# Layer 0's attention: scores one head at a time, and each product with v cut into two pieces that lie in two steps

## The chip, the cores and the metric

The kernel runs on one core of one Trainium2 chip. The metric is the device time in microseconds of one execution, and the median of three executions is quoted.

## What is computed

Two transformer layers on a (2, 1024, 128) input; attention and a feed-forward part are added in parallel in each. The change touches the attention of layer 0 alone:

```python
x = L0_attn_x
xn = _layernorm(x, axis=-1)
x = x + _L0_attn_ref(xn, ...) + _L0_ffn_ref(xn, ...)
xn = _layernorm(x, axis=-1)
x = x + _L1_attn_ref(xn, ...) + _L1_ffn_ref(xn, ...)

# _L0_attn_ref: B, T, C = 2, 1024, 128; H = 16 heads of D = 8
qkv = x @ W_attn + b_attn
att = jnp.einsum('bhtd,bhsd->bhts', q, k) / jnp.sqrt(D)
att = att + _alibi_causal_mask(T, H, x.dtype)[None]
att = jax.nn.softmax(att, axis=-1)
y = jnp.einsum('bhts,bhsd->bhtd', att, v)
return y.reshape(B, T, C) @ W_proj + b_proj
```

## The kernel before

Layer 0's attention is done in 8 groups (2 batches, 4 heads each at a time). A group has 10 units, UNITS, and each unit is one step of a loop of 80 steps; the text calls a group's steps u0 to u9. u0 to u2 make the first 512 queries, u3 to u9 the last 512. A unit holds up to 512 columns of queries against one block of 128 keys: u0 and u3 to u7 have one segment of 512, u1 and u8 have two (384 and 128), u2 and u9 one of 256.

In a step TensorE computes the scores of the group's 4 heads (`scores`, line 651, bf16; q and k carry the ALiBi terms and the row maximum as extra rows, 55 in all). Heads 0 and 2 lie in rows 0 to 63 of the array, heads 1 and 3 in rows 64 to 127, so that two neighbours can run side by side. The scores go to three PSUM banks in turn: score k of the whole run uses bank k % 3 and waits until exponential k - 3 has been read. ScalarE takes the exponential of each score (line 1402) into `prob`, which has 3 slots, GpSimd sets what lies above the diagonal to zero (line 1533), and `pv` multiplies the result with v (line 669, float32, 16 output rows for each head, the four heads in four column strips of the array), always into bank 7. After u2 and after u9 `acc` has ScalarE copy bank 7 to `yacc` (line 1391). The next product, that of u3 or u0, overwrites bank 7 and waits for that copy (`s_acc`).

Beside this each step has items from a list (ITEMS, in general two for a step, one for each half of the step) that work one group ahead. A max item is a round of score products for the row maximum (line 583, and line 587 in the two of nine rounds that hold the diagonal) into two of four further banks, which VectorE reduces (line 1088). Item k waits for the reduction of item k - 2. A group has 18 max items. A turn item transposes the finished maxima (line 635), ScalarE copies them to `mrow` (line 1356), and the sync engine writes them with four DMAs into q_op (line 471, `load_m`). Turn (n, 0) lies in u5, turn (n - 1, 1) in u1. Behind the four DMAs of turn (n, 0) the same queue issues the four loads of q_op and k_op for the group after it (line 463, `load_ops`), and for these the first max item of that group waits, which lies in u9. In the last group there are no max items; the tail's items (transposes, projection) lie beside its steps.

The engines' instructions stand in program order, written out by hand in one function for each engine; only semaphores order them against one another. SyncE's queue carries all DMAs.

Of the kernel before, what the change touches and what calls it, by code (L numbers as in the profile page):

```python
# [22 lines left out]
P = 128  # L23
# [9 lines left out]
GH = 4  # L33
# [74 lines left out]
P_SLOTS = 3  # L108
# [70 lines left out]
def build(nc, x, w, wright, consts, alibi_q, alibi_k, masks, chosen, out):  # L179
    alibi_q, alibi_k, masks, chosen = (v.bitcast(BF16) for v in (alibi_q, alibi_k, masks, chosen))  # L180
    with ExitStack() as ctx:
# [340 lines left out]
        def _(pe):  # L522
# [33 lines left out]
            def item(k):  # L556
# [14 lines left out]
                elif kind == "max":  # L571
# [8 lines left out]
                    for t, (i, j, nb, at) in enumerate(ROUNDS[r]):  # L580
                        for odd in range(2):
                            rows = rows_of(odd, MAX_K)
                            last = mm(PS[:, ring + odd, P * at:P * (at + nb)], q_op[rows, slot, pair, P * i:P * i + P],  # L583
                                      k_op[rows, slot, pair, P * j:P * (j + nb)], start=(t == 0), stop=(r not in DIAGONALS),
                                      skip_group_check=True)
# [71 lines left out]
            def pv(s):  # L657
                n, u = divmod(s, NU)
                b, g = GROUPS[n]
                half, segs = UNITS[u]  # L660
                pe.wait_ge(s_exp, GH * (s + 1))
                pe.wait_ge(s_tri, TRI[s])
                if u in (0, 3):
                    pe.wait_ge(s_acc, 1 + 2 * n + (u == 3))
                at = 0
                for j, i0, nn in segs:
                    c0 = P * i0 - SPAN * half
                    for h in range(GH):
                        last = mm(PS[STRIP * h:STRIP * h + VW, 7, c0:c0 + nn], vaug[:, TPB * b + j, g * GH + h, :],  # L669
                                  prob[:, s % P_SLOTS, h, at:at + nn], start=(j == 0),  # L670
                                  stop=(u in (2, 9)), skip_group_check=True)
                    at += nn
                last.then_inc(s_pv, 1)
# [47 lines left out]
            for s in range(NSTEP + 1):  # L721
                beside = items_of_step(s) if s < NSTEP else ()
                for half in range(2):
                    if s < NSTEP:
                        scores(s, range(GH // 2 * half, GH // 2 * (half + 1)))
                    for k in (beside[:len(beside) // 2], beside[len(beside) // 2:])[half]:
                        item(k)
                if s:
                    pv(s - 1)
# [580 lines left out]
        def _(a):  # L1310
# [82 lines left out]
            for s in range(NSTEP + 1):  # L1393
# [4 lines left out]
                for half in range(2):  # L1398
                    for h in range(GH // 2 * half, GH // 2 * (half + 1)) if s < NSTEP else ():
# [3 lines left out]
                                       ACT.Exp).then_inc(s_exp, 1)  # L1403
                    for k in (beside[:len(beside) // 2], beside[len(beside) // 2:])[half]:
                        item(k)
                if s:
                    acc(s - 1)
# [272 lines left out]
```

## Time and profile before

| what | value |
|---|---|
| median of 3 runs | 536.89 us (532.29 to 537.02) |
| profiled execution: time, span | 539.22 us, 537.5 us |
| TensorE busy (x4188) | 424.8 us, 79% |
| VectorE busy (x584) | 351.0 us, 65% |
| ScalarE busy (x471) | 241.2 us, 45% |
| GpSimd busy (x309) | 195.6 us, 36% |
| mean granted clock of TensorE | 0.939 |
| line 1402, exponentials, x320 | 159.9 us busy, 73.5 us idle before them |
| line 1088, reductions of maxima, x144 | 171.9 us busy, 49.8 us idle before them |
| line 669, products with v, x768 | 83.7 us busy |
| line 651, scores, x384 | 61.7 us busy, 43.8 us idle before them |

The attention of layer 0 lies between about 43 and 304 us of the span, 80 steps. Busy times are unions for each engine and a mean over stages; matmuls are pipelined, and each float32 matmul stands as two records.

### The profile page before, as it was taken

To read this page: it belongs to the slowest core of one execution; us is meant where nothing else is said; L and a number is where in the kernel's file an instruction comes from. 1 tells how busy PE (TensorE), PEld (TensorE's weight loads), DVE (VectorE), ACT (ScalarE), POOL (GpSimd) and SP (SyncE) were. 2 spreads that over 40 slices of the span, in tenths; PEclk is the share of its full clock that TensorE was granted. 3 is DMA by queue.
4 is the path that set the end of the run, shared out by engine and by line. 5 is a ranking of instruction groups with operands and counts; after the bars stand their busy time and mean duration, and the time that the engine had idled before them with its cause. 6 is when DMAs were issued, how large, how long until landed. Compare 5 with 4: busy or idle time off the path is not lost.

```text
span 537.5 us, 10677 instructions
## 1 busy us (share of the span) xinstructions
PE 424.8 (79%) x4188; PEld 197.1 (37%) x4188; DVE 351.0 (65%) x584; ACT 241.2 (45%) x471; POOL 195.6 (36%) x309
## 2 busy tenths in 40 slices
PE   6797788878788787788686896596888798869766
PEld 3253213232222222221242552344544463446544
DVE  5878768778788878786255285876368627862640
ACT  1575476877776777767566210431111111121220
POOL 3022515252322222130210146638338716780530
PEclk9997789999999999998799597888999998999989
DMA  7632240414202020200000032221022102300000
GB/s 225 225 77 68 78 159 16 169 30 164 64 3 66 2 68 2 67 2 2 2 1 1 1 117 79 79 80 41 1 79 99 40 2 79 119 21 1 22 3 20
DMA packets 19094, 31.92 MB, mean 59 GB/s; under 512 B 2544, under 2 KB 7120, under 8 KB 18724
## 3 DMA queue, kind: packets, MB, share of 16 engines
q1 hardware_dynamic: 19044, 31.23, 18.1%
q8 instruction: 34, 0.56, 0.4%
q14 instruction: 16, 0.13, 0.1%
HBM read 13.20 MB, written 8.06 MB: 40 GB/s over the span
## 4 chain that ended last, share of the span: by engine, by line
PE 35%; issue 18%; POOL 18%; ACT 10%; DVE 8%; DMA 6%; SPq 5%; POOLq 0%; ACTq 0%; DVEq 0%
PE PS L669 9%; ACT prob L1402 7%; PE PS L651 6%; POOL vdec L1562 6%; POOL qr L1554 5%; POOL xn L1571 5%; DVE pmax L1088 4%; DMA k_op<-k_scr 4%; SPq L471 3%; PE PS L583 3%; PE PS L587 2%; PE PS L784 2%; POOL kr L1554 1%; PE PS L540 1%; PE PS L880 1%
## 5 line engine op out<-in xcount | busy, mean ns | idle before, releaser
L1088 DVE TENSOR_REDUCE pmax<-PS 128x8 f32<-128x1024 f32 x144 | 171.9, 1222 | 49.8 <-PE PS L583 33.4
L1402 ACT ACTIVATE prob<-PS 128x512 f32<-128x512 f32 (+1 forms) x320 | 159.9, 552 | 73.5 <-PE PS L651 70.5
L1533 POOL TENSOR_SCALAR_AFFINE_SELECT prob<-prob 128x512 f32<-128x512 f32 x64 | 39.9, 635 | 179.7 <-ACT prob L1402 179.7
L651 PE MATMUL PS<-q_op,k_op 55*128 55x512 bf16 (+3 forms) x384 | 61.7, 342 | 43.8 <-ACT prob L1402 41.1
L669 PE MATMUL PS<-prob,vaug 128*16 128x512 f32 (+3 forms) x768 | 83.7, 526 | 0.0
L583 PE MATMUL PS<-k_op,q_op 52*128 52x128 bf16 (+3 forms) x576 | 58.5, 279 | 9.1 <-DVE pmax L1088 4.6
L651 PEld LDWEIGHTS PS<-q_op,k_op 55*128 55x128 bf16 x384 | 18.4, 94 | 125.4 <-ACT prob L1402 108.7
L1571 POOL TENSOR_TENSOR xn<-state,c_sb 128x512 f32<-128x512 f32 x28 | 29.3, 1046 | 81.5 <-DVE state L1271 56.4
L1426 ACT COPY vk<-PS 128x512 f32<-128x512 f32 x16 | 9.4, 585 | 86.5 <-PE PS L795 86.5
L784 PE MATMUL PS<-xnT,w_sb 128*128 128x512 f32 x80 | 44.0, 650 | 0.6 <-DVE by_sin L1238 0.6
L1554 POOL TENSOR_TENSOR qr<-qr,turned 128x512 f32<-128x512 f32 x32 | 40.0, 1269 | 4.9 <-DMA turned<-by_sin 4.8
L1271 DVE TENSOR_TENSOR state<-PS,xn 128x512 f32<-128x512 f32 x28 | 19.3, 688 | 30.4 <-PE PS L864 21.5
L1562 POOL TENSOR_TENSOR vdec<-vk,c_sb 128x256 f32<-128x256 f32 x64 | 37.2, 613 | 1.4 <-ACT vk L1426 1.4
L1457 ACT COPY oT<-PS 128x512 f32<-128x512 f32 x32 | 17.2, 589 | 39.0 <-PE PS L853 39.0
L583 PEld LDWEIGHTS PS<-k_op,q_op 52*128 52x128 bf16 x576 | 24.8, 96 | 22.8 <-DVE pmax L1088 9.4
L1234 DVE TENSOR_TENSOR qr<-PS,c_sb 128x512 f32<-128x512 f32 x32 | 21.9, 683 | 13.0 <-PE PS L784 12.9
L1245 DVE TENSOR_TENSOR sm<-PS,c_sb 128x512 f32<-128x512 f32 x32 | 20.6, 685 | 13.8 <-PE PS L812 13.1
L812 PE MATMUL PS<-qr,kr 64*64 64x256 f32 x256 | 19.2, 414 | 12.4 <-DVE state L1271 6.3
L880 PE MATMUL PS<-oT,w_sb 128*128 128x256 f32 x128 | 28.7, 382 | 0.0
L836 PE MATMUL PS<-sm,vk 64*64 64x256 f32 x256 | 19.7, 426 | 11.0 <-DVE sm L1245 11.0
L669 PEld LDWEIGHTS PS<-prob,vaug 128*16 128x16 f32 x768 | 15.2, 97 | 34.5 <-ACT prob L1402 21.7
L1238 DVE TENSOR_TENSOR by_sin<-PS,c_sb 128x512 f32<-128x512 f32 x40 | 27.1, 678 | 0.0
(181 smaller groups left out, 527.2 us busy)
## 6 DMA issues: line engine op xcount, KB each, us to landing
turned<-by_sin SPq DMA_DIRECT2D x80, 128.0 KB, 2.0
k_op<-k_scr SPq DMA_DIRECT2D x14, 220.0 KB
q_op<-q_scr SPq DMA_DIRECT2D x14, 208.0 KB
c_sb<-const_dram SPq DMA_DIRECT2D x1, 2060.0 KB, 7.2
w_sb<-w_dram SPq DMA_DIRECT2D x1, 1876.5 KB, 7.6
q_scr<-part_a SPq DMA_DIRECT2D x6, 256.0 KB, 3.5
k_scr<-part_a SPq DMA_DIRECT2D x6, 256.0 KB, 3.8
q_scr<-part_b SPq DMA_DIRECT2D x6, 256.0 KB, 3.4
```

Source lines behind the costliest of these rows:

```text
L583: last = mm(PS[:, ring + odd, P * at:P * (at + nb)], q_op[rows, slot, pair, P * i:P * i + P], k_op[rows, slot, pair, P * j:P * (j + nb)], ...
L651: last = mm(PS[:, (GH * s + h) % ST_BANKS, at:at + nn], k_op[rows, slot, h // 2, P * j:P * j + P], q_op[rows, slot, h // 2, P * i0:P * i0 ...
L669: last = mm(PS[STRIP * h:STRIP * h + VW, 7, c0:c0 + nn], vaug[:, TPB * b + j, g * GH + h, :], prob[:, s % P_SLOTS, h, at:at + nn], start=( ...
L784: mm(bank01(("p", i, m)), w, xnT[:, SPAN * i:SPAN * i + SPAN], start=True, stop=True).then_inc(s_pj, 1)
L880: last = mm(by_half(ps)[:, :, s, :], wo[:, C * kt:C * kt + C], by_half(oT[:, i % 2, kt, :])[:, :, s, :], start=False, stop=(s == 1 and kt ...
L1088: vec.tensor_reduce(pmax[:, of_pair, at:at + step * (TPS - 1) + 1:step], both.rearrange("p a (b c) -> p a b c", c=P), AX.X, ALU.max).then_ ...
L1238: vec.tensor_tensor(by_sin[:, n % SIN_SLOTS, :], PS[:, k % 2, :], K["sin"][:, t], ALU.mult).then_inc(s_pj_free, 1)
L1402: sca.activation(prob[:, s % P_SLOTS, h, 0:UNIT_W[u]], PS[:, k % ST_BANKS, 0:UNIT_W[u]], ACT.Exp).then_inc(s_exp, 1)
L1533: po.affine_select(out=blk, in_=blk, compare_op=ALU.is_ge, fill=0.0, base=0, pattern=[[0, GH], [1, P]], channel_multiplier=-1).then_inc(s_ ...
L1554: po.tensor_tensor(dst, dst, turned[:, n % TURN_SLOTS, :], ALU.add).then_inc(done, 1)
L1562: po.tensor_tensor(vdec[:, c % 2, g, :, :], vk[:, c % 2, D1 * g:D1 * g + D1].rearrange("p (o e) -> p o e", o=1).broadcast_to([P, HPG, D1]) ...
L1571: po.tensor_tensor(faded, state[:, u % STATES, :, :], fade, ALU.mult).then_inc(s_faded, 1)
```

## The change

TensorE's step is written in another order. Before: scores of heads 0 and 1, the first item, scores of heads 2 and 3, the second item, the whole product with v of the step before. Now: score 0, first item, score 1, the second piece of the product of two steps ago, score 2, second item, score 3, the first piece of the product of the step before. A product of two segments is cut between them, one of a single segment in the middle of its columns (256 and 256, or 128 and 128). The products of a max item take the odd head first: ahead of the item stands an even head's score, behind it an odd head's. ScalarE's copy of bank 7 for step s - 2 stands behind the exponential of head 2 of step s; before, the copy for step s - 1 stood at the end of step s. The loops run one step longer.

```diff
@@ item(), TensorE
-                        for odd in range(2):
+                        for odd in (1, 0):
...
@@ pv(), TensorE
-            def pv(s):
+            def pv(s, piece):
...
-                pe.wait_ge(s_exp, GH * (s + 1))
-                pe.wait_ge(s_tri, TRI[s])
-                if u in (0, 3):
-                    pe.wait_ge(s_acc, 1 + 2 * n + (u == 3))
-                at = 0
-                for j, i0, nn in segs:
+                if piece == 0:
+                    pe.wait_ge(s_exp, GH * (s + 1))
+                    pe.wait_ge(s_tri, TRI[s])
+                    if u in (0, 3):
+                        pe.wait_ge(s_acc, 1 + 2 * n + (u == 3))
+                j, i0, nn = segs[0]
+                pieces = segs if len(segs) == 2 else [(j, i0, nn // 2), (j, i0 + nn // 2 // P, nn // 2)]
+                at = pieces[0][2] if piece else 0
+                for j, i0, nn in pieces[piece:piece + 1]:
...
-                last.then_inc(s_pv, 1)
+                if piece:
+                    last.then_inc(s_pv, 1)
@@ the loop over steps, TensorE
-            for s in range(NSTEP + 1):
+            for s in range(NSTEP + 2):
...
-                        scores(s, range(GH // 2 * half, GH // 2 * (half + 1)))
+                        scores(s, [GH // 2 * half])
                     for k in (beside[:len(beside) // 2], beside[len(beside) // 2:])[half]:
                         item(k)
-                if s:
-                    pv(s - 1)
+                    if s < NSTEP:
+                        scores(s, [GH // 2 * half + 1])
+                    at, piece = ((s - 2, 1), (s - 1, 0))[half]
+                    if 0 <= at < NSTEP:
+                        pv(at, piece)
@@ the loop over steps, ScalarE
+                        if h == 2 and s >= 2:
+                            acc(s - 2)
...
-                if s:
-                    acc(s - 1)
+                if s >= NSTEP:
+                    acc(s - 2)
```

TensorE before, u6 and the start of u7 of a group: two scores (L651), a max item on the diagonal (L583, L587), two scores, a max item, the product with v (L669).

```order
L651 MATMUL PS<-q_op,k_op 128x512 [waits s_exp]
L651 MATMUL PS<-q_op,k_op 128x512
L583 MATMUL PS<-k_op,q_op 128x128 [waits s_used0]
L583 MATMUL PS<-k_op,q_op 128x128 x7
L587 MATMUL PS<-masks_sb 128x512 x2
L651 MATMUL PS<-q_op,k_op 128x512 [waits s_exp]
L651 MATMUL PS<-q_op,k_op 128x512
L583 MATMUL PS<-k_op,q_op 128x512 [waits s_used1]
L583 MATMUL PS<-k_op,q_op 128x512
L669 MATMUL PS<-prob,vaug 16x512 [waits s_tri,s_exp]
L669 MATMUL PS<-prob,vaug 16x512 x3
L651 MATMUL PS<-q_op,k_op 128x512 [waits s_exp]
```

TensorE now, at the same place (the product with v is L673):

```order
L651 MATMUL PS<-q_op,k_op 128x512 [waits s_exp]
L583 MATMUL PS<-k_op,q_op 128x128 [waits s_used0]
L583 MATMUL PS<-k_op,q_op 128x128 x7
L587 MATMUL PS<-masks_sb 128x512 x2
L651 MATMUL PS<-q_op,k_op 128x512 [waits s_exp]
L673 MATMUL PS<-prob,vaug 16x256 x4
L651 MATMUL PS<-q_op,k_op 128x512 [waits s_exp]
L583 MATMUL PS<-k_op,q_op 128x512 [waits s_used1]
L583 MATMUL PS<-k_op,q_op 128x512
L651 MATMUL PS<-q_op,k_op 128x512 [waits s_exp]
L673 MATMUL PS<-prob,vaug 16x256 [waits s_tri,s_exp]
L673 MATMUL PS<-prob,vaug 16x256 x3
```

Each score stands alone now, and a piece of 256 columns stands behind the second and the fourth.

TensorE before, in u1: the turn item (L635), two scores in two segments, a max item, the product of u0 with its wait for the copy of bank 7 (`s_acc`), the next step's first score.

```order
L635 MATMUL PS<-masks_sb,mpart 12x128 [waits s_mpart,s_used1]
L635 MATMUL PS<-masks_sb,mpart 12x128 x3
L651 MATMUL PS<-q_op,k_op 128x384 [waits s_exp]
L651 MATMUL PS<-q_op,k_op 128x384
L651 MATMUL PS<-q_op,k_op 128x128 x2
L583 MATMUL PS<-k_op,q_op 128x128 [waits s_used0]
L583 MATMUL PS<-k_op,q_op 128x128
L583 MATMUL PS<-k_op,q_op 128x384 x2
L669 MATMUL PS<-prob,vaug 16x512 [waits s_acc,s_tri,s_exp]
L669 MATMUL PS<-prob,vaug 16x512 x3
L651 MATMUL PS<-q_op,k_op 128x256 [waits s_exp]
```

TensorE now, from the piece of u9 that follows the second score of u1 to the first score of u2:

```order
L673 MATMUL PS<-prob,vaug 16x128 x4
L651 MATMUL PS<-q_op,k_op 128x384 [waits s_exp]
L651 MATMUL PS<-q_op,k_op 128x128
L583 MATMUL PS<-k_op,q_op 128x128 [waits s_used0]
L583 MATMUL PS<-k_op,q_op 128x128
L583 MATMUL PS<-k_op,q_op 128x384 x2
L651 MATMUL PS<-q_op,k_op 128x384 [waits s_exp]
L651 MATMUL PS<-q_op,k_op 128x128
L673 MATMUL PS<-prob,vaug 16x256 [waits s_acc,s_tri,s_exp]
L673 MATMUL PS<-prob,vaug 16x256 x3
L651 MATMUL PS<-q_op,k_op 128x256 [waits s_exp]
```

The wait for `s_acc` stands at the same place of u1 as before, at its end, but the product that the copy reads ends in the middle of u1 now, where it ended with u0 before.

ScalarE before, u0, u1 (`prob` are the exponentials, `mrow` the turned maxima, `yacc` the copy of bank 7):

```order
L1402 ACTIVATE prob<-PS 128x512 [waits s_st,s_pv]
L1402 ACTIVATE prob<-PS 128x512 [waits s_st] x3
L1391 COPY yacc<-PS 128x512 [waits s_pv]
L1402 ACTIVATE prob<-PS 128x512 [waits s_st,s_pv]
L1402 ACTIVATE prob<-PS 128x512 [waits s_st]
L1356 COPY mrow<-PS 12x512 [waits s_item]
L1402 ACTIVATE prob<-PS 128x512 [waits s_st] x2
```

ScalarE now, the same two steps:

```order
L1409 ACTIVATE prob<-PS 128x512 [waits s_st,s_pv]
L1409 ACTIVATE prob<-PS 128x512 [waits s_st] x3
L1409 ACTIVATE prob<-PS 128x512 [waits s_st,s_pv]
L1409 ACTIVATE prob<-PS 128x512 [waits s_st]
L1363 COPY mrow<-PS 12x512 [waits s_item]
L1409 ACTIVATE prob<-PS 128x512 [waits s_st]
L1398 COPY yacc<-PS 128x512 [waits s_pv]
L1409 ACTIVATE prob<-PS 128x512 [waits s_st]
```

The copy of bank 7 has moved from ahead of u1's first exponential to behind its third, and behind the copy of the maxima.

## Rows read from the trace of the kernel before

**Rows 1.** Waits, 40 to 305 us: engine, line <- releaser: total us, times, longest

```profile
ACT prob L1402 <- PE PS L651: 70.5, 86, 4.1
PE PS L651 <- ACT prob L1402: 41.1, 62, 3.4
...
PE PS L583 <- DMA k_op<-k_scr: 2.8, 4, 1.0
```

**Rows 2.** Timeline of TensorE in u6: start us, us, what, [idle before <- releaser]

```profile
190.04 0.39 PE L583 MATMUL PS<-k_op,q_op 52*128 52x128 bf16 x8
...
191.04 0.39 PE L651 MATMUL PS<-q_op,k_op 55*128 55x512 bf16 x2
191.25 0.40 PE L583 MATMUL PS<-k_op,q_op 52*128 52x512 bf16 x2
191.58 1.05 PE L669 MATMUL PS<-prob,vaug 128*16 128x512 f32 x8
192.56 0.39 PE L651 MATMUL PS<-q_op,k_op 55*128 55x512 bf16 x2
```

**Rows 3.** Timeline of ScalarE, u0 to u5 of the sixth group

```profile
201.86 2.24 ACT L1402 ACTIVATE prob<-PS 128x512 f32<-128x512 f32 x4 [0.93 <-PE PS L651]
204.38 0.58 ACT L1391 COPY yacc<-PS 128x512 f32<-128x512 f32 x1 [0.28 <-PE PS L669]
204.87 1.09 ACT L1402 ACTIVATE prob<-PS 128x512 f32<-128x512 f32 x2
205.83 0.56 ACT L1356 COPY mrow<-PS 12x512 bf16<-12x512 bf16 x1
...
207.52 0.66 ACT L1402 ACTIVATE prob<-PS 128x256 f32<-128x256 f32 x2 [0.17 <-PE PS L651]
...
213.34 2.27 ACT L1402 ACTIVATE prob<-PS 128x512 f32<-128x512 f32 x4
216.12 1.08 ACT L1402 ACTIVATE prob<-PS 128x512 f32<-128x512 f32 x2 [0.51 <-PE PS L651]
217.09 0.56 ACT L1356 COPY mrow<-PS 12x512 bf16<-12x512 bf16 x1
```

**Rows 4.** Timeline of VectorE, from u9 of the fifth group on

```profile
200.13 3.49 DVE L1088 TENSOR_REDUCE pmax<-PS 128x8 f32<-128x1024 f32 x3 [1.40 <-PE PS L587]
```

**Rows 5.** Chain of waits, u6 to u9 of the fifth group

```profile
193.16 5.79 DMA k_op<-k_scr
...
199.09 0.40 PE PS L583 x8
```

**Rows 6.** Timeline of TensorE: the DMA's wait in u9 of the sixth group

```profile
227.90 0.40 PE L583 MATMUL PS<-k_op,q_op 52*128 52x128 bf16 x8 [0.98 <-DMA k_op<-k_scr]
```

**Rows 7.** Timeline of TensorE in the last group: a product of 256 columns, the next scores

```profile
276.35 0.63 PE L669 MATMUL PS<-prob,vaug 128*16 128x256 f32 x8
...
276.91 0.39 PE L651 MATMUL PS<-q_op,k_op 55*128 55x512 bf16 x2
```

**Rows 8.** Timeline of ScalarE in the last group, u3 and u4

```profile
274.26 2.24 ACT L1402 ACTIVATE prob<-PS 128x512 f32<-128x512 f32 x4 [1.76 <-PE PS L651]
...
277.52 2.24 ACT L1402 ACTIVATE prob<-PS 128x512 f32<-128x512 f32 x4
```

**Rows 9.** Stretches: length, busy us (x) of PE, PEld, DVE, ACT, POOL; PEclk, DMA

```profile
225.00:230.00 5.00, 3.91 (x48) 1.43 (x48) 3.33 (x4) 2.86 (x7) 2.57 (x8) 1.00 0.25 57
...
242.90:246.30 3.40, 3.38 (x15) 0.44 (x16) 1.66 (x2) 1.45 (x3) 0.00 (x0) 0.50 0.00 0
...
260.00:265.00 5.00, 4.16 (x29) 2.18 (x27) 0.00 (x0) 2.68 (x5) 0.19 (x1) 0.50 0.01 2
```

**Rows 10.** Timeline of TensorE, just ahead of the last stretch of rows 9

```profile
259.81 0.37 PE L635 MATMUL PS<-masks_sb,mpart 128*12 128x128 bf16 x3 [1.67 <-POOL mpart L1510]
```

**Rows 11.** Timeline of ScalarE, u4 and u5 of the seventh group

```profile
242.15 1.12 ACT L1402 ACTIVATE prob<-PS 128x512 f32<-128x512 f32 x2
...
246.43 1.08 ACT L1402 ACTIVATE prob<-PS 128x512 f32<-128x512 f32 x2 [1.80 <-PE PS L651]
```

More of the change, by code:

```diff
@@ L669, in pv @@
                         last = mm(PS[STRIP * h:STRIP * h + VW, 7, c0:c0 + nn], vaug[:, TPB * b + j, g * GH + h, :],
-                                  prob[:, s % P_SLOTS, h, at:at + nn], start=(j == 0),
+                                  prob[:, s % P_SLOTS, h, at:at + nn], start=(j == 0 and piece == 0),
                                   stop=(u in (2, 9)), skip_group_check=True)
-                    at += nn
-                last.then_inc(s_pv, 1)
+                if piece:
+                    last.then_inc(s_pv, 1)
             def unit_b(k, part):
@@ L1391, in acc @@
                     sca.copy(yacc[:, n, SPAN * half:SPAN * half + SPAN], PS[:, 7, :]).then_inc(s_acc, 1)
-            for s in range(NSTEP + 1):
+            for s in range(NSTEP + 2):
                 u = s % NU
```

## The prediction

> **What bounds the kernel now.** First I read the page, then the waits, then one step on TensorE, then the engines that hand work to one another, last the chain of waits at the seams between groups. In the attention no engine is full. ScalarE waits 70.5 us for scores and TensorE 41.1 us for exponentials [rows 1]: each waits for the other in turn. The reader is to see the loop in one step [rows 2]. Scores of heads 2 and 3 start at 191.04, the second item 0.21 us later, the product with v at 191.58, and it holds TensorE until the next step's scores at 192.56, 0.98 us. ScalarE needs 2.24 us for four exponentials; in a plain step 0.51 us of idle stand in front of its first exponential [rows 3], so it takes 2.75 us, and this idle is what the block costs. That is what the change can win: with the block halved and scores spread evenly, three banks are enough for ScalarE, and the next limit is VectorE with two reductions a step, 3.49 us for three or 1.16 us each [rows 4], so 2.33 us.
>
> The reader is to see a second loop as well, at the seam between groups. In u5 ScalarE copies the turned maxima, and only then does the queue issue four DMAs and four loads; the last load takes 5.79 us, and the first max item of the group after, in u9, starts at 199.09 [rows 5]. From the copy at 217.09 [rows 3] to the same item at 227.90 [rows 6] it is 10.8 us. TensorE stood still for this DMA in four groups, up to 1.0 us each [rows 1]. So in those groups the steps u5 to u9 are already as long as the DMA chain allows, and faster steps there only make that wait longer. What counts for them is the other part of the round: from the item in u9 (199.09) to the copy in u5 (217.09), 18.0 us.
>
> **The price of cutting a product.** A product of 256 columns takes 0.56 us up to the next scores, one of 512 takes 0.98 [rows 2, 7]. So two halves cost 1.12, 0.14 more. A piece that follows an item starts 0.33 us behind the item's start, scores that precede an item only 0.21 [rows 2]: going over from scores to the product costs 0.12, and there is one more such passage. Together TensorE gets 0.26 us more for each step. A plain step is then 0.21 + 0.33 + 0.56, twice, or 2.2 us, and is hidden by VectorE's 2.33; a step with an item on the diagonal has 0.45 more (scores follow such an item at most 1.0 us behind its start, 190.04 to 191.04 [rows 2], with a wait in it; I take 0.87, less the overlap of a score) and is bound by TensorE at 2.65.
>
> The Trainium skill says in TensorEngine Tiling, Key Properties, that a change of the tiling mode drains the engine. Scores use the array in two row halves, the products in four column strips, so the change doubles these drains; the 0.12 and 0.14 above agree with such a drain and give it a size. Without it, with 0.26 less in each of u9, u0 and u2 of seven groups, the forecast would be some 4 us lower.
>
> The swapped order of the odd and the even head costs nothing in itself: the score ahead runs beside the item's first product, the score behind beside its last. If a bank isn't free, the item's last product runs alone, 0.21 us, which lies in a wait anyway.
>
> **The copy of bank 7.** The product of u0 (and of u3) must wait for the copy of bank 7. Before, that copy was made at the end of u0, a whole step ahead of the product at the end of u1. Now it stands behind the third exponential of u1, and the product still stands at the end of u1. From u1's first exponential, the copy of the maxima starts at 0.96 and takes 0.56, the third exponential starts some 1.42 behind the first and takes 0.55, the copy itself 0.58 [rows 3]: its end is at 2.55 us; with 0.12 to pass it on, the piece starts at 2.7. TensorE is there about 0.9 us after that first exponential, since score 3 only needs the first one to be read. It stands still for almost 2 us, with the piece (0.56), the next step's first score and its max item queued behind the wait; ScalarE runs dry meanwhile (0.5 us), and VectorE too. In u4 there is no copy of maxima, the wait is some 1.4 us, and the step is 2.25 + 0.12 + 0.56 + 0.49 (scores to first exponential) = 3.4 us against 2.78 before (213.34 to 216.12).
>
> **The seam, walked through.** From the item in u9 as zero, with these prices, the first exponential of u0 comes at 3.4 (before 2.77), of u1 at 5.9 (5.78: the copy is no longer ahead of it), of u2 at 9.5 (8.43), of u3 at 12.6, of u4 at 14.8 (14.25), of u5 at 18.2 (17.03) [all "before" from rows 3, less 199.09]. The copy of the maxima comes at 19.2 against 18.0: **+1.2 us** a group, at the one stretch that the DMA chain doesn't cover.
>
> **The sum.**
> - Stretch u9 to u5: five rounds of the DMA loop x 1.2 = +6.0, and the groups outside it (first, seventh) about +1.1 each: +8.2.
> - u5 to u9 where no load is waited for (first and seventh group): 2.7 + 2.65 + 2.33 + 2.33 + 2.6 = 12.65 us against four plain steps of 2.75 and a shorter u9, about 13.4: -0.75 x 2 = -1.5. In the fourth group VectorE has the feed-forward's scales beside its reductions: nothing.
> - Last group: no reductions, steps near 3.26 (274.26 to 277.52 [rows 8]). TensorE waits for a bank in them and could fill that with a piece, some 0.4 in five of the steps, but pays 0.26 and the wait for the copy twice: -1.
> - TensorE's clock. In u9 TensorE would wait for the loads some 2.2 us in place of 1.0, in u1 almost 2 us for the copy. The trace has a wait of 1.67 us [rows 10], and the granted clock stands at 0.5 (1.2 GHz) right behind it [rows 9]; behind the 1.0 us of the DMA wait at 227.90 it stayed at 2.4 GHz [rows 6, 9]. With the lower level from 242.9 to 246.3 [rows 9] u4 of the seventh group took 4.3 us, 242.15 to 246.43 [rows 11], against 2.78, so one fall costs about 1.5. There are eleven places (four DMA waits, seven u1); I count four falls and take off the one that stands in the trace now: +4.5. Bounds: -1.5 (none) to +15 (all).
>
> Total +10.2. The profiled execution took 539.2 us, 2.3 above the median; set on the median 536.9 this gives **547 us**.
>
> **Rivals.**
> - *The same waits, but the clock holds.* +5.7, 542.6 us (539 to 545). For it: the waits of up to 1.0 us in the steps now leave the clock at 2.4 GHz, 225 to 230 among them [rows 9]. Against: the wait of 1.67 us and what came behind it [rows 9, 10].
> - *Faster: the wait for the copy is hidden.* If ScalarE is far enough ahead when TensorE comes to the piece (because TensorE itself is late, with drains dearer than 0.12, or the items held up by VectorE), u1 and u4 lose nothing, and the stretch u9 to u5 goes down toward VectorE's work: 11 reductions x 1.16 + 2.5 for the start and the turn items = 15.3 in place of 18.0. A third to all of these 2.7 us seven times, with -1.5 and -1: 515 to 528 us, say 524. It decides where TensorE reaches the piece less than 0.5 us ahead of the copy's end. Against: score 3 waits only for exponential 0 of its step, and behind it nothing stands before the piece.
> - *Nothing that counts moves.* The DMA loop holds the round, the wait for the copy costs what the spread scores win in u0 to u4: +0 there, -1.5 and -1: 534 us.
> - *Half clock that stays.* If TensorE's work in u9 to u2 at the lower level takes the whole time, one fall brings the next: over 553 us.
>
> **Chances.** Forecast 0.45 (541 to 553), clock holds 0.22, hidden wait 0.17, nothing moves 0.12, half clock that stays 0.04. A measurement tells 1% (5.4 us, 531.5 to 542.3) from no change. The clock case lies across the upper bound, half on each side; that makes slower 0.58, same 0.26, faster 0.16. The range leaves out the hidden wait and the lasting half clock: 532 to 554.
>
> **What would show it.** Behind the copy of bank 7 in u1 and u4 a product with v waits for ScalarE's line of that copy, about 1.9 and 1.4 us (none of that before): right. Steps u6 to u8 near 2.3 to 2.65 us, against 2.75: the mechanism of the spread scores. The wait of TensorE for the loads in u9 up from 1.0 to some 2.2 us, and 30 us from such an item to the next (28.8 before, 199.09 to 227.90): the DMA loop. A mean granted clock below 0.939. I am wrong if the round between two such items falls below 28.5 us, if the product isn't seen waiting for the copy, or if steps stay at 2.75.

## The result, and the profile after

The changed kernel is **slower: 549.98 us** against 536.95 us of the kernel before on the same chip, ratio 1.027 (95% interval 1.021 to 1.033). A second measurement on another chip gave 1.025 (1.016 to 1.034). Its profiled execution took 553.81 us with a span of 552.1 us, 14.6 us above the profiled span before. Ratios here leave out executions more than 1.5% above the fastest of their kernel, so they differ by up to a per cent or so from the quotient of two medians.

The page of the changed kernel, busy times, the granted clock in 40 slices of the span, and the groups of the exponentials (L1409), of the product with v (L673) and of the scores (L651):

```profile
PE 460.7 (83%) x4700; PEld 216.6 (39%) x4700; DVE 349.9 (63%) x584; ACT 243.8 (44%) x471; POOL 195.9 (35%) x309
...
PEclk9997589989999998989789897898999999989958
...
L1409 ACT ACTIVATE prob<-PS 128x512 f32<-128x512 f32 (+1 forms) x320 | 164.0, 558 | 86.8 <-PE PS L651 84.6
L673 PE MATMUL PS<-prob,vaug 128*16 128x256 f32 (+2 forms) x1280 | 99.8, 386 | 15.2 <-ACT yacc L1398 14.9
L651 PE MATMUL PS<-q_op,k_op 55*128 55x512 bf16 (+3 forms) x384 | 106.6, 345 | 3.5 <-ACT prob L1409 2.8
```

VectorE and ScalarE do the same work as before; TensorE is busy 36 us longer, and ScalarE still waits for scores, longer than before. The scores' own busy time, 61.7 us before, is 106.6 us now: scores that had run side by side, two at a time, now come one at a time. The waits view of the changed kernel, 40 to 320 us (engine, line <- releaser: total, times, longest), answers to [rows 1]:

```profile
ACT prob L1409 <- PE PS L651: 84.6, 107, 3.2
...
PE PS L673 <- ACT yacc L1398: 14.9, 14, 1.3
```

TensorE's wait for exponentials, 41.1 us in [rows 1], is all but gone. In its place stands a wait that did not exist: the product with v waits for the copy of bank 7, 14 times. TensorE's timeline of the changed kernel, from u9 of the fifth group to u9 of the sixth (start, us, what, idle before and its releaser):

```profile
206.65 0.40 PE L583 MATMUL PS<-k_op,q_op 52*128 52x128 bf16 x8 [1.39 <-DMA k_op<-k_scr]
...
207.72 1.02 PE L673 MATMUL PS<-prob,vaug 128*16 128x256 f32 x8
...
216.85 0.62 PE L673 MATMUL PS<-prob,vaug 128*16 128x256 f32 x8 [1.30 <-ACT yacc L1398]
...
225.00 0.62 PE L673 MATMUL PS<-prob,vaug 128*16 128x256 f32 x8 [0.98 <-ACT yacc L1398]
...
228.17 0.39 PE L651 MATMUL PS<-q_op,k_op 55*128 55x512 bf16 x1
...
230.12 0.39 PE L651 MATMUL PS<-q_op,k_op 55*128 55x512 bf16 x1
...
231.22 0.39 PE L651 MATMUL PS<-q_op,k_op 55*128 55x512 bf16 x1
...
232.32 0.39 PE L651 MATMUL PS<-q_op,k_op 55*128 55x512 bf16 x1
...
237.33 0.40 PE L583 MATMUL PS<-k_op,q_op 52*128 52x128 bf16 x8 [1.43 <-DMA k_op<-k_scr]
```

A plain step takes 2.20 us (230.12 to 232.32, from the third score of u6 to that of u7), and u6 as a whole, with its item on the diagonal, 3.05 us (228.17 to 231.22). But u1 and u4 stand still behind the copy, and both items in u9 wait longer for the loads than in [rows 6]. The piece at 207.72 takes 1.02 us where its like takes 0.62: the clock had fallen (a granted clock of 0.52 from 207.7 to 211). ScalarE's timeline, u1 and u5 of the same group:

```profile
215.20 0.56 ACT L1363 COPY mrow<-PS 12x512 bf16<-12x512 bf16 x1
215.66 0.58 ACT L1409 ACTIVATE prob<-PS 128x512 f32<-128x512 f32 x1
216.15 0.56 ACT L1398 COPY yacc<-PS 128x512 f32<-128x512 f32 x1
...
227.11 0.56 ACT L1363 COPY mrow<-PS 12x512 bf16<-12x512 bf16 x1
```

The copy of bank 7 ends at 216.71 and the piece starts 0.14 us behind it. In the rest of the text a **round** is the time from one copy of bank 7 after u9 to the next; the second round begins with the first such copy, at 87.51 before and 93.18 now, and the stretch ahead of it is called the first. The stretches view (length, busy us of PE, PEld, DVE, ACT, POOL, then granted clock, DMA share, GB/s) of the kernel before: the third, the sixth and the seventh round, and the part behind the attention, which the change doesn't touch:

```profile
115.92:145.08 29.16, 23.76 (x242) 7.82 (x240) 24.19 (x23) 21.50 (x44) 10.63 (x25) 1.00 0.33 106
204.38:233.19 28.81, 22.67 (x234) 6.99 (x232) 22.07 (x21) 21.50 (x44) 7.30 (x19) 1.00 0.12 32
233.19:266.93 33.74, 26.08 (x218) 8.40 (x216) 18.89 (x21) 22.08 (x46) 7.62 (x19) 0.85 0.01 2
...
303.48:537.50 234.02, 184.06 (x2128) 112.48 (x2128) 134.78 (x284) 42.12 (x78) 114.89 (x133) 0.94 0.14 51
```

The same of the changed kernel:

```profile
123.90:154.06 30.16, 26.64 (x304) 9.77 (x304) 24.10 (x23) 21.69 (x45) 10.17 (x23) 1.00 0.31 103
...
216.15:246.83 30.68, 26.97 (x296) 9.20 (x296) 21.92 (x21) 21.81 (x45) 7.31 (x18) 0.94 0.12 30
246.83:278.70 31.87, 27.94 (x273) 9.89 (x274) 17.47 (x20) 21.73 (x46) 7.30 (x18) 0.85 0.01 3
...
312.57:552.10 239.53, 189.09 (x2128) 114.04 (x2128) 134.70 (x284) 42.12 (x78) 114.93 (x133) 0.92 0.14 50
```

So the 14.6 us of the two profiled spans are: 9.1 us up to the last copy of bank 7 (303.48 to 312.57), and 5.5 us behind it, in instructions that are the same in both kernels, at a clock of 0.92 in place of 0.94. At full clock the third round costs 1.0 us more; the sixth costs 1.9 more, at 0.94.

### The profile page after: what moved, and what is told of

Its sections match the earlier page's. It is cut to its first block, busy times and chain, and to the rows that moved or that the text cites. A ratio compares the mean times of both kernels' runs of the same rounds, so it can differ in the third digit from the quotient of the medians.

```text
span 552.1 us, 11558 instructions
## 1 busy us (share of the span) xinstructions
PE 460.7 (83%) x4700; PEld 216.6 (39%) x4700; DVE 349.9 (63%) x584; ACT 243.8 (44%) x471; POOL 195.9 (35%) x309
## 4 chain that ended last, share of the span: by engine, by line
PE 41%; POOL 18%; issue 17%; ACT 10%; DVE 7%; DMA 5%; SPq 1%; POOLq 0%; ACTq 0%; DVEq 0%
PE PS L673 10%; PE PS L651 7%; ACT prob L1409 7%; POOL vdec L1571 5%; POOL qr L1563 5%; POOL xn L1580 5%; PE PS L583 4%; DMA k_op<-k_scr 4%; DVE pmax L1095 3%; PE PS L587 3%; PE PS L887 2%; PE PS L791 2%; PE PS L540 2%; POOL kr L1563 1%; ACT yacc L1398 1%
## 5 line engine op out<-in xcount | busy, mean ns | idle before, releaser
L1409 ACT ACTIVATE prob<-PS 128x512 f32<-128x512 f32 (+1 forms) x320 | 164.0, 558 | 86.8 <-PE PS L651 84.6
L673 PE MATMUL PS<-prob,vaug 128*16 128x256 f32 (+2 forms) x1280 | 99.8, 386 | 15.2 <-ACT yacc L1398 14.9
L651 PE MATMUL PS<-q_op,k_op 55*128 55x512 bf16 (+3 forms) x384 | 106.6, 345 | 3.5 <-ACT prob L1409 2.8
L583 PE MATMUL PS<-k_op,q_op 52*128 52x128 bf16 (+3 forms) x576 | 80.4, 290 | 10.3 <-DMA k_op<-k_scr 5.6
L651 PEld LDWEIGHTS PS<-q_op,k_op 55*128 55x128 bf16 x384 | 29.1, 95 | 90.7 <-ACT prob L1409 52.8
L673 PEld LDWEIGHTS PS<-prob,vaug 128*16 128x16 f32 x1280 | 21.7, 95 | 58.2 <-ACT prob L1409 30.3
L791 PE MATMUL PS<-xnT,w_sb 128*128 128x512 f32 x80 | 43.5, 644 | 0.9 <-DVE by_sin L1245 0.9
L1278 DVE TENSOR_TENSOR state<-PS,xn 128x512 f32<-128x512 f32 x28 | 19.2, 687 | 32.0 <-PE PS L871 23.0
L583 PEld LDWEIGHTS PS<-k_op,q_op 52*128 52x128 bf16 x576 | 29.1, 98 | 22.6 <-issue 10.5
L887 PE MATMUL PS<-oT,w_sb 128*128 128x256 f32 x128 | 31.0, 404 | 0.0
L843 PE MATMUL PS<-sm,vk 64*64 64x256 f32 x256 | 21.1, 452 | 11.4 <-DVE sm L1252 11.4
L887 PEld LDWEIGHTS PS<-oT,w_sb 128*128 128x128 f32 x128 | 25.7, 203 | 7.5 <-issue 3.8
```

The source lines that it names most:

```text
L651: last = mm(PS[:, (GH * s + h) % ST_BANKS, at:at + nn], k_op[rows, slot, h // 2, P * j:P * j + P], q_op[rows, slot, h // 2, P * i0:P * i0 ...
L791: mm(bank01(("p", i, m)), w, xnT[:, SPAN * i:SPAN * i + SPAN], start=True, stop=True).then_inc(s_pj, 1)
L887: last = mm(by_half(ps)[:, :, s, :], wo[:, C * kt:C * kt + C], by_half(oT[:, i % 2, kt, :])[:, :, s, :], start=False, stop=(s == 1 and kt ...
L1409: sca.activation(prob[:, s % P_SLOTS, h, 0:UNIT_W[u]], PS[:, k % ST_BANKS, 0:UNIT_W[u]], ACT.Exp).then_inc(s_exp, 1)
```

## The experiments

Each ratio is against the kernel before, in runs on the same chip. The kernel before had a median of 540.39 us beside runs 1 to 4, 538.67 beside runs 5 to 8 and 537.66 beside runs 9 to 12, where the expectations reckon with 537; so the ratios are what answers them.

**1. The copy one exponential earlier** (changed kernel).

```diff
-                        if h == 2 and s >= 2:
+                        if h == 1 and s >= 2:
                             acc(s - 2)
```

> The changed kernel with one edit: ScalarE copies bank 7 behind the exponential of head 1 of a step, ahead of the copy of the maxima, instead of behind that of head 2. Theory (the wait of the first piece for this copy is the main cost): the copy ends 1.0 us earlier in u1 and 0.55 us earlier in u4, so the waits of 1.30 and 0.98 us fall to about 0.3 and 0.4, and with eight groups the time falls by 8 x 1.4 = 11 us, to 539 (537 to 543). Rival (the price lies in the extra passages between scores and products and in the clock): the waits shrink, but the time falls by 3 us at most, 547 or more. Under both the steps u6 to u8 stay at 2.2 to 2.6 us.

Measured 543.06 us, 1.011 (1.007 to 1.016). Waits view, 40 to 310 us:

```profile
PE PS L673 <- ACT yacc L1398: 5.5, 13, 0.7
PE PS L583 <- DMA k_op<-k_scr: 5.0, 4, 1.3
```

Its third round, in the stretches view:

```profile
117.02:146.09 29.07, 26.78 (x309) 9.86 (x307) 24.12 (x22) 21.59 (x46) 10.26 (x24) 1.00 0.33 106
```

That is 1.09 us below the changed kernel's at the same clock, 0.09 below the kernel before. The waits shrank as the theory said, and the time came down by most of what it said. Nothing but the place of the copy differs (in u1 it now stands ahead of the copy of the maxima too), so the place of the copy costs 1.6% (1.027 to 1.011).

**2. The loads ahead of the maxima's write** (changed kernel). SyncE issues the four loads of the group after the next ahead of the four DMAs of the turned maxima, so that the loads no longer wait for the copy of the maxima.

```diff
-                load_m(n, 0)
...
+                load_m(n, 0)
```

> The changed kernel with one edit in SyncE's queue: the loads of q_op and k_op for group n + 1 are issued ahead of the four small DMAs of turn (n, 0), not behind them. Theory (the seam's DMA chain eats what the steps u5 to u9 win): the wait of 1.4 us in u9 goes in all four groups, the falls of the clock behind it (three in the trace) as well, and the time falls by 4 x 1.4 to 4 x 1.4 + 3 x 1.5, to 540 to 544, say 541. Rival (the loads are not what holds the groups; something else, the small DMAs of the maxima or VectorE, comes next): 547 or more, with a wait of the same length at another place of u9 to u3.

Measured 544.62 us, 1.015 (1.008 to 1.022). No product of L583 waits for a DMA in the attention, and the copy's wait is unchanged (14.9 us, 14 times, longest 1.3). Its third round:

```profile
120.68:149.35 28.67, 26.46 (x304) 9.75 (x304) 24.09 (x23) 21.70 (x45) 10.06 (x23) 1.00 0.35 108
```

1.49 us less than the changed kernel's. The loads' loop was real and cost about 1.2% in the changed kernel (1.027 to 1.015; the two intervals just touch), at the short end of what was expected.

**3. The same edit in the kernel before.**

> The same edit of SyncE's queue in the kernel before. Theory: it waits only 0.4 to 1.0 us for the loads in four groups, 2.8 us in all, so 534 (532 to 536). The difference between this gain and that of the changed kernel is what the DMA chain took from the change. Rival (the wait is made up for elsewhere): 537, no change.

Measured 536.06 us, 0.999 (0.994 to 1.004): the rival's "no change". The attention ends 3.9 us earlier in its trace (299.57 against 303.48), which the whole time doesn't show. Its third round:

```profile
114.87:143.40 28.53, 23.56 (x242) 7.80 (x240) 24.19 (x23) 21.50 (x44) 10.61 (x25) 1.00 0.35 108
```

That is 0.63 us less than before, where the changed kernel gained 1.49. The loop is dearer where the rest of the round is fast enough to run into it.

**4. Single scores alone** (kernel before): odd head first in the items, scores one by one, the product whole and the copy where it was.

```diff
-                        scores(s, range(GH // 2 * half, GH // 2 * (half + 1)))
+                        scores(s, [GH // 2 * half])
...
                         item(k)
+                    if s < NSTEP:
+                        scores(s, [GH // 2 * half + 1])
                 if s:
                     pv(s - 1)
```

> The first half of the change alone: scores one by one around the items, odd head first in an item, but the product with v whole at the end of the next step and the copy of bank 7 where it was. Theory (single scores are good by themselves, cutting the product and moving the copy are what costs): no wait for the copy, no added passages; score 2 and the second item no longer wait for exponential 0, so the product starts about 0.2 us earlier and ScalarE's idle of 0.51 us a step falls to about 0.3. With the DMA chain still in u9, 4 to 6 us faster than the kernel before, 531 to 533. Rival (single scores cost TensorE more than they give, since two of them no longer run side by side wherever an item waits): 538 or more.

Measured 535.50 us, 0.991 (0.983 to 0.999), the gain that the theory named. Its third round:

```profile
115.03:143.61 28.58, 26.50 (x241) 8.89 (x240) 24.01 (x23) 21.07 (x46) 10.79 (x24) 1.00 0.31 108
```

0.58 us less than before, but TensorE is busy 26.50 us of it, where it was 23.76: single scores buy an even supply of scores with TensorE's slack. The last group, held by no reductions, went from 36.55 to 33.94 us at the same clock of 0.87. The seventh round went from 33.74 to 29.99, but at 0.92 in place of 0.85.

**5. Both repairs** (changed kernel with the edits of 1 and 2).

> The changed kernel with both repairs: bank 7 copied behind the exponential of head 1, and the loads for the next group issued ahead of the small DMAs of turn (n, 0). Theory (wait for the copy and DMA chain are separate prices): the ratios of the two single repairs to the changed kernel, 1.0113/1.0272 and 1.0151/1.0272, multiply to 0.973, so 0.9994 of the kernel before, 537 beside 537 (within 0.7%). Rival (once the loads wait for nothing, steps run at VectorE's and TensorE's pace throughout and the spread scores pay fully): 0.985 or less, 529. Rival two (the same microseconds counted twice): 1.008 or more.

Measured 532.56 us, 0.984 (0.976 to 0.992): below the 0.9994 that was expected; the first rival's bound held. Its third round:

```profile
116.08:143.76 27.68, 26.61 (x309) 9.84 (x307) 24.10 (x22) 21.60 (x45) 10.19 (x24) 1.00 0.35 112
```

It is 2.48 us below the changed kernel's; the two edits gave 1.09 and 1.49 apart, 2.58 in sum. In this round they add up. The whole time is less sure than its ratio looks: eight of the ten executions took 532.0 to 534.4 us, two took 522.5 and 528.5.

**6. The wait for the loads filled** (changed kernel): six products of 512 columns with no use, ahead of the wait, from the third group on. They keep TensorE at work while the DMA runs.

```diff
+                        for _ in range(6 if n > 1 else 0):
+                            mm(PS[:, ring, :].rearrange("p (b c) -> p b c", c=P), ident_b,
+                               causal_b.rearrange("p (o c) -> p o c", o=1).broadcast_to([P, TPS, P]),
+                               start=True, stop=True, skip_group_check=True)
                         pe.wait_ge(s_op[slot], OP_EACH * (n // OP_SLOTS + (slot > 0)))
```

> The changed kernel with six added bf16 products of 512 columns (into the free banks of the first max item of each group from the third group on, overwritten by the item itself) ahead of that item's wait for the loads. They take 6 x 0.21 = 1.3 us where TensorE waits 1.4 us, so they cost nearly nothing; they only keep TensorE at work. Theory (falls of the clock behind these waits, three in the trace, are a price): no fall in u9 and u0, 3 x 1.5 = 4.5 us less, ratio to the kernel before 1.019. Rival (the falls are spread by chance and cost what waits would cost anyway): 1.027, or a little more for the added work.

Measured 549.21 us, 1.029 (1.023 to 1.035). Its fifth and sixth rounds:

```profile
188.27:217.32 29.05, 26.77 (x302) 9.41 (x302) 21.83 (x21) 21.70 (x45) 7.34 (x18) 1.00 0.12 32
217.32:247.55 30.23, 26.84 (x302) 9.42 (x302) 21.84 (x21) 21.71 (x45) 7.33 (x18) 1.00 0.12 31
```

Both rounds keep the full clock, where the changed kernel's stood at 0.94, and the fifth is 1.6 us shorter, the sixth 0.45; but the whole didn't get faster, with other rounds at 0.94 or 0.95 (30.54, 33.68, 30.12 us). The traced execution, 543.88 us, was moreover the fastest of six by 4.9 us, with a mean clock of 0.955; the other five had 0.935 to 0.938. As a remedy the filling is worth nothing here.

**7. Single scores with the loads early** (edits of 4 and 2 on the kernel before).

> The kernel with scores one by one, the product whole and the copy where it was, and with the loads for the next group issued ahead of the small DMAs. Theory: its waits for the loads, 5.3 us in all, and the falls of the clock behind them go: 0.991 less 1 to 1.5%, so 0.978, 525 beside 537. Rival (the time comes back as a wait for the small DMAs in u3 or for VectorE): 0.989 or more.

Measured 526.45 us, 0.987 (0.981 to 0.994), between the two values expected. Its third round, the shortest of all:

```profile
114.66:142.09 27.43, 26.36 (x241) 8.93 (x240) 24.01 (x23) 21.07 (x46) 10.67 (x24) 1.00 0.35 112
```

The attention ends 9.2 us earlier than in run 4's trace (286.60 against 295.78), where run 3's ended 3.9 earlier than that of the kernel before. Not all of the 9.2 is the loop: the sixth, seventh and last rounds ran at a higher clock here than in run 4 (1.00, 1.00, 0.90 against 0.94, 0.92, 0.87). The second, third and fifth rounds are at full clock in all four traces, and in these three together the open loop is worth 4.26 us here and 2.35 us in run 3: single scores had made the steps fast enough to run into it. The ratios of runs 4 and 7 themselves overlap.

**8. Cut product and late copy under paired scores** (changed kernel with scores in pairs and the even head first).

```diff
-                        scores(s, [GH // 2 * half])
+                        scores(s, range(GH // 2 * half, GH // 2 * (half + 1)))
...
-                    if s < NSTEP:
-                        scores(s, [GH // 2 * half + 1])
```

> The second half of the change alone: the product cut and the copy of bank 7 moved as in the change, but scores of two heads together ahead of the items and the even head first in an item, as before. Theory (cutting and the late copy are the price, single scores the gain, and they add): single scores gave 0.9% by themselves, so without them 1.027 x 1.009 = 1.036, 556 beside 537. Rival (once the block is halved, the pairing no longer matters): 1.027, 551. Rival two (the price is in the single scores together with the pieces): 1.01 or less.

Measured 540.52 us, 1.011 (1.001 to 1.020), near the second rival's bound. I had expected this to be the slowest, with the costs kept and the gain of the single scores given up. So single scores, worth 0.9% alone, *cost* 1.6% beside the late copy and the cut. Four more runs on one chip went after that.

**9. The changed kernel again.**

> The changed kernel once more, beside the three others on one chip. Theory: its ratio of 1.027 stands (1.022 to 1.033), so that single scores and cut pieces together cost 1.7% more than cut pieces under paired scores (1.0105 so far). Rival: the two ratios lie within 0.8% of each other when measured on one chip; then the gap between them was chance, and the cut and the late copy account for the whole slowdown.

Measured 553.41 us, 1.025 (1.016 to 1.034): the ratio stands.

**10. Single scores and a late copy, the product whole** (run 4 with the copy moved).

```diff
+                        if h == 2 and s >= 2:
+                            acc(s - 2)
...
-                if s:
-                    acc(s - 1)
+                if s >= NSTEP:
+                    acc(s - 2)
```

> Kernel before with single scores (odd head first in the max items), the product whole at the end of the next step, and ScalarE's copy of bank 7 moved behind the exponential of head 2 of step s for step s - 2, as in the changed kernel. Against the run with single scores alone (0.991) only the copy has moved. Theory: the product of u0 and of u3 waits for it as in the changed kernel, 1 to 1.9 us, 14 times; in u1 this lies in the part of the round that counts, 7 x 1.3 = 9 us, in u4 it lies there too, and a part of it is taken back by the wait for the loads: ratio 1.008 to 1.02. What is left to the changed kernel (1.027) is the price of the cut with single scores, some 0.7 to 1.9%. Rival one: the whole product ends later than a first half, so the copy's wait is covered and the ratio is at most 0.996; then the cut makes all of the slowdown. Rival two: 1.025 or more, and the cut costs nothing.

Measured 554.34 us, 1.028 (1.022 to 1.033): rival two. The whole slowdown is there without any cut. Its waits view:

```profile
PE PS L669 <- ACT yacc L1393: 18.4, 15, 1.7
```

Its third round:

```profile
122.58:153.17 30.59, 26.07 (x240) 9.02 (x240) 24.00 (x23) 21.22 (x46) 10.17 (x23) 1.00 0.30 101
```

Against run 4 the copy's place costs 3.7% of the time (0.991 to 1.028), 2.0 us of a round at full clock. That is a longer move than in run 1: past three exponentials and the copy of the maxima.

**11. Cut product under paired scores, copy early** (run 8 with the edit of 1).

> The run with paired scores, cut product and late copy (1.0105), with the copy one exponential earlier, behind that of head 1. What is left against the kernel before is the cut and little of the copy's wait (5.5 us in all were left in the changed kernel with this edit). Theory: the copy's wait is what that run lost, and the cut under paired scores is hidden: 0.997 to 1.003. Rival: the cut costs 0.26 us in each of 80 steps wherever the loads' loop doesn't hide it (50 steps, 13 us): 1.01 or more, no lower than with the late copy.

Measured 529.36 us, 0.985 (0.979 to 0.991): the cut costs nothing, and both values expected were too high. Its third round:

```profile
116.55:146.00 29.45, 25.27 (x309) 8.87 (x307) 24.11 (x22) 21.51 (x45) 10.12 (x23) 1.00 0.33 105
```

It is 0.3 us longer than before; the fourth and the fifth, also at full clock, are 0.75 and 0.6 shorter. Its attention ends 5.9 us earlier than that of the kernel before (297.59 against 303.48), and 4.8 us of that lie in the last group (36.55 to 31.72, at 0.87 and 0.89).

**12. Run 8 again.**

> Paired scores, cut product, late copy, once more. Theory: 1.010 as before (1.005 to 1.016), 9 us below the changed kernel. Rival as for the run of the changed kernel: 1.02 or more.

Measured 544.47 us, 1.003 (0.997 to 1.009). The gap to the changed kernel stands, 2.2% on one chip by the ratios and 1.6% by the medians (544.47 and 553.41); the twelve executions spread from 532.4 to 548.0 us. The two traces of this one kernel show what the clock alone does. Stretches of run 8, the third round:

```profile
116.61:146.70 30.09, 25.04 (x304) 8.79 (x304) 24.11 (x23) 21.63 (x45) 10.20 (x23) 1.00 0.32 102
```

Of run 12, the third round and two microseconds near its start:

```profile
117.11:149.23 32.12, 27.84 (x304) 9.82 (x304) 24.16 (x23) 21.72 (x45) 10.16 (x23) 0.89 0.30 96
...
119.00:121.00 2.00, 2.00 (x15) 1.17 (x8) 1.39 (x2) 1.06 (x4) 1.26 (x3) 0.51 0.33 57
```

TensorE's timeline in run 8, the wait for the copy in u1:

```profile
117.32 0.62 PE L673 MATMUL PS<-prob,vaug 128*16 128x256 f32 x8 [1.27 <-ACT yacc L1396]
```

The same in run 12:

```profile
117.81 0.63 PE L673 MATMUL PS<-prob,vaug 128*16 128x256 f32 x8 [1.27 <-ACT yacc L1396]
```

The same instructions, the same wait of 1.27 us; behind it the clock stays at 2.4 GHz in one execution and falls to 1.2 GHz in the other (0.51 from 119 to 121), and the round is 2.0 us longer. The fifth round repeats it (28.90 us at 1.00, 30.97 at 0.89). The two executions are of different chips; but the twelve of run 12, on one chip, had mean clocks from 0.922 to 0.963 too.

**The runs side by side.** The third round is at full clock in all of these, so it shows the kernels without the clock. The copy of bank 7 stands at the end of u0 and u3 (early), behind the exponential of head 1 in u1 and u4 (head 1), or behind that of head 2 (late):

| kernel | scores | product | copy | loads | third round, us | TensorE busy in it, us | ratio |
|---|---|---|---|---|---|---|---|
| before | pairs | whole | early | late | 29.16 | 23.76 | 1 |
| run 3 | pairs | whole | early | early | 28.53 | 23.56 | 0.999 |
| run 4 | single | whole | early | late | 28.58 | 26.50 | 0.991 |
| run 10 | single | whole | late | late | 30.59 | 26.07 | 1.028 |
| run 11 | pairs | cut | head 1 | late | 29.45 | 25.27 | 0.985 |
| run 8 | pairs | cut | late | late | 30.09 | 25.04 | 1.011, 1.003 |
| run 1 | single | cut | head 1 | late | 29.07 | 26.78 | 1.011 |
| changed | single | cut | late | late | 30.16 | 26.64 | 1.027, 1.025 |
| run 2 | single | cut | late | early | 28.67 | 26.46 | 1.015 |
| run 5 | single | cut | head 1 | early | 27.68 | 26.61 | 0.984 |
| run 7 | single | whole | early | early | 27.43 | 26.36 | 0.987 |

What single scores cost beside the late copy isn't in this round (30.09 and 30.16). It is in the first group and in the clock. Stretches of the changed kernel, from 44 us to the first copy after u9, and ten microseconds within:

```profile
44.00:93.18 49.18, 40.99 (x369) 13.31 (x367) 34.86 (x34) 28.41 (x57) 13.97 (x30) 0.76 0.26 79
...
60.00:70.00 10.00, 8.33 (x71) 2.85 (x71) 5.47 (x6) 3.81 (x9) 5.04 (x14) 0.61 0.21 66
```

In run 8, with the copy at the same place:

```profile
60.00:70.00 10.00, 7.01 (x90) 2.19 (x87) 8.26 (x8) 6.45 (x14) 5.17 (x9) 1.00 0.62 201
```

Its first stretch takes 43.5 us (44 to 87.47), and 43.9 in run 12; the changed kernel takes 49.2, and 50.7 in run 9. These 5.3 to 7.2 us are on average more than half of the gap in the attention, which ends at 296.94 and 305.41 in the two traces of run 8's kernel and at 312.57 and 310.13 in the two of the changed one. The other traces narrow it down. From 72 to 80 us, behind the first wait for the copy in u4, run 2 (the same order on TensorE and ScalarE as in the changed kernel) and run 1 (the copy behind head 1) show:

```profile
72.00:80.00 8.00, 8.00 (x54) 2.12 (x50) 2.45 (x2) 3.94 (x8) 0.00 (x0) 0.58 0.58 193
```

```profile
72.00:80.00 8.00, 8.00 (x92) 2.53 (x92) 5.66 (x5) 7.07 (x14) 0.08 (x1) 1.00 0.56 192
```

All four traces with single scores, the cut and the late copy are below full clock there (0.79, 0.51, 0.58 and 0.79 in the changed kernel and runs 9, 2 and 6), with a first stretch of 49.1 to 50.7 us. Runs 1 and 5, with the copy behind head 1, and runs 8, 10, 11 and 12, which lack the cut or the single scores, all stand at 1.00, with first stretches of 44.8, 45.3, 43.5, 47.9, 42.1 and 43.9. So this loss goes with the whole combination, in every trace; why the clock falls there in just these kernels is not shown.

## Why the prediction came out as it did

The forecast was 547.0 us; 549.98 were measured. By its own steps:

- **The price of cutting** (0.26 us for each step). The piece does take 0.56 us up to the next scores, and a plain step 2.20 us, as said. The step with an item on the diagonal was put at 2.65 us and takes 3.05, where it took 2.75 before (189.81 to 192.56): scores follow such an item 1.08 us behind its start (228.17 to 229.25), not 0.87, and the 1.0 us read off [rows 2] held no wait, since the trace lists none at 191.04. The three steps u6 to u8 took 7.45 us together, near the 7.3 forecast and below the 8.26 of before (189.81 to 198.07). But as a term of the sum it fell: run 11 has every cut and is 1.5% faster than the kernel before, and run 10 has none and is as slow as the changed kernel. TensorE's busy time grows by 1.5 us in a round (23.76 to 25.27, run 11), out of its slack. With it falls the weight I gave to the drain that the Trainium skill names in TensorEngine Tiling, Key Properties: whatever a drain costs TensorE, no run here shows that it costs the kernel anything. What did fill TensorE I had at nothing: single scores, +2.7 us of busy time in a round (23.76 to 26.50, run 4).
- **The copy of bank 7.** The mechanism was right and is the largest part: 0.985 to 1.007 (the mean of runs 8 and 12) under paired scores, 1.011 to 1.026 under single ones, 0.991 to 1.028 with a whole product and a longer move. The size of one wait was not: 1.30 and 0.98 us where I had 1.9 and 1.4. The copy ended about where I put it, at 216.71, and the piece started 0.14 behind it against 0.12; but TensorE reached the wait at 215.55, only 1.16 us ahead of the copy's end, where I had 1.65.
- **The seam.** Item in u9 to copy of the maxima in u5: 20.46 us (206.65 to 227.11) in place of the 19.2 forecast, with a clock fall right at its start; less the 1.6 us that a fall costs (below) it is 18.8, against 18.0 before. The loop's own part, copy to item, is 10.22 (227.11 to 237.33) against 10.8. From item to item 30.68, forecast 30. The wait for the loads reached 1.5 us, not 2.2. At full clock the third round is 1.0 us longer where I had 1.2, and run 9's round from 94.71 to 123.80 takes 29.09, 0.68 more than the 28.41 (87.51 to 115.92) before.
- **The DMA loop eats the gain of u5 to u9.** Shown by run 2 (1.027 to 1.015 with the loop opened) and by run 7 against run 4.
- **The last groups.** For the seventh group I had +1.1 and -0.75, for the last -1. The seventh round went down by 1.9 us at the same clock of 0.85, so the spread scores gave more there than I had; the last group ran from its first exponential, 9.9 us late, to its end, 9.1 us late: -0.8.
- **The clock.** I put a fall at 1.5 us and counted four. Two executions of the changed kernel differ by 1.63 us in the second round (30.72 at 0.94, 29.09 at 1.00) and by 1.66 in the third; three of the five rounds that had none before now have one, in each execution. So size and count were about right: 3 x 1.65 = 4.9 against +4.5. Run 8, a sister kernel with the same waits for the copy, shows that the clock can hold at them, as one rival had it; which of the two comes is not set by the code alone.
- **Not in the sum.** The first group lost 3.5 us up to the second group's first exponential, 1.3 of them ahead of the attention and the rest with a half clock that stayed on for long: the fourth rival's mechanism in one group. And 5.5 us came behind the attention. There the kernels are the same, and the stretch took between 231.3 us (run 10) and 239.8 us (run 12), so one trace can't put them down to the change; run 9 shows 239.5 again.

Attention alone gave +9.1 us in the trace where the sum said +10.2. The number was near in part by luck: an overrated term (the cut, and the copy's wait by a third) stood against two that weren't there (the first group, the part behind the attention).

**Open** stays why run 1 is 1.011 and run 11 is 0.985. Both traces end the attention alike (298.04 and 297.59); behind it run 1 takes 237.5 us and run 11 232.7, at clocks of 0.92 and 0.95. In these two traces it is the clock in unchanged code, but the two traced executions are only 5.3 us apart (537.26 and 531.99), where the medians are 13.7 apart (543.06 and 529.36, on two chips). So the larger part of the gap lies in executions without a trace, and what single scores have to do with it was not settled.

**The best version** is one of runs 5, 7 and 11, 0.984 to 0.987, whose intervals overlap; all three are faster than both kernels. On the chip that they share, all four executions of run 7 (525.1 to 527.7 us) lie below nine of the ten of run 5. Run 7 has the smallest edit, and run 11 leaves TensorE the most slack. Run 11 with the loads early was not tried.

## What to carry to other kernels

A buffer that one engine must empty before another can go on belongs early in the emptying engine's order: one exponential of lateness (0.5 us, with a copy of the maxima 1 us) was worth 1.6% here, and what splitting a step gives by feeding an engine evenly is lost if the same edit moves such a copy. When an edit feeds an engine better, look for the loop that it runs into next (here a DMA chain issued behind a late copy), since the two paid more together than apart. And compare kernels in stretches at the same granted clock before comparing their spans, since one fall cost a round 1.6 to 2.0 us here, as much as the largest of the edits.

## What the runs showed of the hardware

- The same program with the same waits to the hundredth of a microsecond ran a round at 1.00 in one execution and at 0.89 in another, on another chip, 30.09 and 32.12 us, and the kernel before alone lay between 530.7 and 544.6 us in 17 runs on one chip. Differences under 1% need many runs.
- Six filling products ahead of a DMA wait kept the full clock in the fifth and sixth rounds, and the time of the kernel did not improve (1.029).
- Four float32 products in column strips between bf16 scores in row halves, cut in two and put twice as often between them, filled 1.5 us more of TensorE's time in a round (23.76 to 25.27) and didn't make the kernel slower (0.985); pairs of scores in different row halves taken apart cost 2.7 us of TensorE's time in a round of 29 us.
